# Taking VectorE out of half of the experts: the up product leaves PSUM on ScalarE and is multiplied in on GpSimd

## What is computed

```python
x = x + attention(layernorm(x))
xf = layernorm(x)                                   # (2048, 128)
weights, idx = gate(xf)                             # softmax, groups of 4, top 2 of 16 experts
combine = (one_hot(idx, 16) * weights[..., None]).sum(1)
h1 = einsum('td,edi->tei', xf, We1) + be1           # 16 experts, 64 wide
h3 = einsum('td,edi->tei', xf, We3) + be3
h = silu(h1) * h3
y = einsum('te,ted->td', combine, einsum('tei,eid->ted', h, We2) + be2)
z = (silu(xf @ ws1 + bs1) * (xf @ ws3 + bs3)) @ ws2 + bs2   # shared experts
x = x + y + z
```

## Time and profile before

| | |
|---|---|
| median of 3 runs | 423.87 us (423.43 to 426.72) |
| the profiled execution's own time | 423.36 us |
| its span, first to last instruction | 421.6 us |
| PE busy | 355.5 us, 84% |
| DVE busy | 311.8 us, 74% |
| ACT busy | 265.1 us, 63% |
| POOL busy | 202.1 us, 48% |
| mean granted TensorE clock | 0.931 of full |

### The profile page before, as it was taken

The page is one execution under the profiler, slowest core; times in us unless marked ns, Lnnn a source line. Parts: engine busy times, 40 slices in busy tenths (PEclk is TensorE's granted clock), DMA queues, the critical chain, the costliest instruction groups (busy, mean ns, idle before and its releaser), DMA issues.

```text
span 421.6 us, 7243 instructions
## 1 busy us (share of the span) xinstructions
PE 355.5 (84%) x2489; PEld 135.9 (32%) x2489; DVE 311.8 (74%) x595; ACT 265.1 (63%) x382; POOL 202.1 (48%) x283
## 2 busy tenths in 40 slices
PE   2743769688988998988789999997998999999796
PEld 2321333233442324322223233232323232434242
DVE  7694994989799997779965696659879336259664
ACT  2413258048779617965389748992884899996480
POOL 7611986786524896622412362311342522559432
PEclk9985659669999989999989999999999999999899
DMA  7232005000500620000290200000000000260171
GB/s 246 91 95 55 2 1 152 2 2 9 145 2 3 150 53 2 2 5 0 72 205 3 76 1 3 0 2 2 1 2 2 26 26 2 67 136 2 45 157 50
DMA packets 16869, 20.01 MB, mean 47 GB/s; under 512 B 1633, under 2 KB 12418, under 8 KB 16706
## 3 DMA queue, kind: packets, MB, share of 16 engines
q1 hardware_dynamic: 15298, 18.24, 17.2%
q10 hardware_dynamic: 1536, 1.31, 1.3%
HBM read 11.95 MB, written 1.18 MB: 31 GB/s over the span
## 4 chain that ended last, share of the span: by engine, by line
PE 46%; DVE 30%; ACT 9%; issue 7%; POOL 4%; DMA 2%; ACTq 1%; DVEq 0%; POOLq 0%
PE psum L986 11%; PE psum L1021 11%; DVE mx_diag L1494 11%; PE psum L966 7%; DVE mx_full L1494 6%; PE psum L1035 5%; ACT probs L1102 4%; PE psum L942 3%; PE psum L905 3%; DMA w_raw<-in_w_attn 2%; PE psum L914 1%; DVE mv L1573 1%; ACT mh L1170 1%; PE psum L936 1%; DMA k_st<-parts 1%
## 5 line engine op out<-in xcount | busy, mean ns | idle before, releaser
L1102 ACT ACTIVATE probs<-psum 128x1024 f32<-128x1024 f32 x144 | 141.0, 1026 | 39.4 <-PE psum L966 38.5
L1494 DVE TENSOR_REDUCE mx_diag<-psum 128x4 f32<-128x512 f32 (+2 forms) x96 | 96.4, 1039 | 29.4 <-PE psum L942 29.1
L1365 POOL TENSOR_TENSOR mh<-mh,mv 128x512 f32<-128x512 f32 x36 | 45.9, 1280 | 81.2 <-DVE mv L1573 81.0
L1494 DVE TENSOR_REDUCE mx_full<-psum 128x2 f32<-128x1024 f32 x64 | 75.6, 1216 | 12.3 <-PE psum L942 12.2
L1355 POOL TENSOR_SCALAR_AFFINE_SELECT probs<-probs 128x256 f32<-128x256 f32 (+1 forms) x112 | 47.7, 444 | 70.3 <-ACT probs L1102 69.0
L986 PE MATMUL psum<-probs,v_ones 128*9 128x512 f32 (+3 forms) x768 | 77.6, 494 | 2.2 <-POOL probs L1355 1.7
L1021 PE MATMUL psum<-x2T,experts 128*128 128x512 f32 x144 | 76.5, 639 | 3.0 <-ACT mv L1161 1.5
L942 PE MATMUL psum<-k_st,q_st 62*128 62x512 bf16 (+3 forms) x384 | 62.7, 358 | 3.9 <-DVE mx_full L1494 2.8
L966 PE MATMUL psum<-q_st,k_st 64*128 64x512 bf16 (+3 forms) x384 | 55.8, 338 | 10.5 <-ACT probs L1102 6.1
L936 PE MATMUL psum<-tabs 64*128 64x64 bf16 (+1 forms) x384 | 26.0, 215 | 21.2 <-DVE mx_diag L1494 8.3
L1573 DVE SCALAR_TENSOR_TENSOR mv<-psum,experts,mv 128x512 f32<-128x512 f32 x36 | 26.5, 745 | 23.3 <-ACT mh L1173 23.3
(11 more groups left out here) (163 smaller groups left out, 388.7 us busy)
## 6 DMA issues: line engine op xcount, KB each, us to landing
comb_b<-combine_scratch SPq DMA_DIRECT2D x32, 256.0 KB, 5.6
q_st<-parts SPq DMA_DIRECT2D x24, 128.0 KB, 2.5
k_st<-parts SPq DMA_DIRECT2D x18, 128.0 KB, 2.4
experts<-in_w_moe SPq DMA_DIRECT2D x1, 1737.0 KB
out<-xs SPq DMA_DIRECT2D x4, 256.0 KB, 2.2
xs<-in_x SPq DMA_DIRECT2D x3, 256.0 KB, 9.7
k_st<-parts ACTq DMA_DIRECT2D x6, 128.0 KB, 4.1
q_st<-maxT SPq DMA_DIRECT2D x32, 4.0 KB
```

The source lines that it names most:

```text
L1102: act.activation(probs[:, n % P_RING, :, :], wpair("scores", (s, i)), ACT.Exp, scale=SCALE).then_inc(exp_done, 1)
L1365: pool.tensor_tensor(t, t, mv[:, at % V_RING, :], ALU.mult).then_inc(gate_done, 1)
L1494: dve.tensor_reduce(dst[:, a % 2, qt, :, pairs[0]:pairs[0] + nm], w, AX.X, ALU.max, negate=True).then_inc(max_free, 1)
```

## The change

For the chunks in `GATED_ON_ACT` (0 and 1, so 18 of the 36 experts) stage `moe_a` leaves DVE. ACT reads u from its bank with an Identity activation that adds the bias, into a new ring `mu` of two buffers; this is now the bank's last read. A third ACT instruction per expert stands where `moe_a` stands in `SCHEDULE`, and it waits until `moe_g` of the expert two before is done, since that frees its buffer. POOL multiplies twice where it multiplied once: `mh` by `mv`, then, behind its own semaphore, `mh` by `mu`. To make room `T_RING` goes from 9 to 8. Chunks 2 and 3 are as before. `plan()` still takes `moe_a` for a stage of DVE, so `SCHEDULE` and the banks are what they were, entry for entry.

```diff
-P_RING, V_RING, T_RING = 6, 4, 9
+P_RING, V_RING, T_RING = 6, 4, 8
+GATED_ON_ACT = (0, 1)
+U_RING = 2
+        mu = sb("mu", [P, U_RING, CH])
+            def biased(x, n):
+                at = UNITS * x + n
+                if at >= U_RING:
+                    act.wait_ge(gate_done, at - U_RING + 1)
+                act.activation(mu[:, at % U_RING, :], wbank("moeU", (x, n)), ACT.Identity, bias=b1[:, unit(n):unit(n) + 1]
+                               ).then_inc(u_read, 1)
+
...
+                elif kind == "moe_a" and arg[0] in GATED_ON_ACT:
+                    biased(*arg)
...
                     pool.wait_ge(u_read, at + 1)
                     t = mh[:, at % T_RING, :]
-                    pool.tensor_tensor(t, t, mv[:, at % V_RING, :], ALU.mult).then_inc(gate_done, 1)
+                    if x in GATED_ON_ACT:
+                        pool.wait_ge(act_t, 2 * at + 2)
+                        link(pool.tensor_tensor(t, t, mv[:, at % V_RING, :], ALU.mult))
+                        pool.tensor_tensor(t, t, mu[:, at % U_RING, :], ALU.mult).then_inc(gate_done, 1)
+                    else:
+                        pool.tensor_tensor(t, t, mv[:, at % V_RING, :], ALU.mult).then_inc(gate_done, 1)
...
-                elif kind == "moe_a":
+                elif kind == "moe_a" and arg[0] not in GATED_ON_ACT:
                     gate_unit(*arg)
```

## The result

The changed kernel takes 447.84 us (median of 4 runs, 445.47 to 450.07), the kernel before 423.94 us beside it (423.43 to 426.72). The ratio is 1.055, with an interval of 1.051 to 1.059: 23.9 us slower. The forecast was 441 with a range of 432 to 448, so the sign is right and the time lies at the upper end of the range. About 7 us are missing in the sum, and what follows is as much about them as about the 17.8 that it had.

What follows compares the result with a forecast made beforehand. No engine bounds the kernel alone; the chain changes hands every few us. 2.7 + 5.0 + 2.0 + 4.0 + 4.1 = 17.8 us on a 421.6 span gave 439.4, then 441.2 as time; forecast 441, range 432 to 448.

Steps and rivals of the forecast that it cites:

- The price of one expert: From the end of `mu` to that of POOL's weighting 4.1 us; experts in a row on POOL 4.0 instead of 2.65.
- A: Chunk 0, experts 0 to 5 (137 to 186 us): +2.7 at the sum of (0,1), +5.0 by that of (0,4).
- B: Rest of chunk 0 (186 to 215 us): late `mu` holds PE, DVE takes part back; +2.0, ends -2.0 and +4.2.
- C: Chunk 1, experts 0 to 3 (236 to 268 us): 1.9 for (1,0) to (1,2), 2.2 for (1,3); together +4.0.
- D: Chunk 1, experts 4 to 6 (290 to 317 us): +4.1 at the sum of (1,6), including 1.2 at (1,4).
- E: Experts (1,7) and (1,8): DVE's lateness, which goes, covers the second product; 0 to within 0.3 us.
- What costs nothing: Chunks 2 and 3 unchanged, `T_RING` 8 leaves distance, and the `gate_done` wait ahead of `mu` is met in time for (0,5).
- added wait: Rival: the `gate_done` wait binds, routing is held, or PE's holes lower the clock; +4, so 445; chance 0.12.
- The rule on the port: Chunk 1's routing under POOL: five instructions held end it near 190, by the rule 191.5; the sum had 0 for it.
- Delays are taken back: Rival: saturated DVE recovers PE's lateness, B gives -2.0, C and D lose only plain products; 434.5; chance 0.14.
- Faster: Rival: PE has slack for every sum and DVE's product leaves the chain, some 5 us; 419; chance 0.03.
- no change: Rival: DVE's gain and POOL's loss cancel, which needs A under 5; chance 0.03.

Runs made afterwards that it cites:

- pool_twice: The kernel before with `T_RING` 8 and, in chunks 0 and 1, a second POOL product into a scratch tile: 445.20 us, ratio 1.051 to the kernel before.
- mu_early: The change with each `mu` instruction right behind the plus-one of its own expert on ACT: 438.55 us, ratio 1.036 to the kernel before.
- chunk 1 alone: The change for chunk 1 only, with chunk 0's nine experts left on DVE: 435.18 us, ratio 1.029 to the kernel before.
- fill_after: The change with PE products of zeros ahead of its wait at six expert sums: 440.64 us, ratio 1.038 to the kernel before.
- two_holds: The kernel before, `T_RING` 8, with an extra POOL product for (0,0) and (0,1): 428.95 us; its pair adds six zero products at (0,1): 425.12 us.
- chunk 0 alone: The change for chunk 0 only, with chunk 1's nine experts left on DVE: 437.07 us, ratio 1.033 to the kernel before.
- five_early: The scheme for experts (0,6), (0,7), (0,8), (1,0), (1,7) only, `mu` right behind the plus-one, others as before: 425.34 us, ratio 1.0035 to the kernel before.
- fill_one: The kernel before with `T_RING` 8 and three PE products of zeros at the sum of (0,1): 424.39 us, ratio 0.9998.
- fill_before: The kernel before with `T_RING` 8 and PE products of zeros, nearly all in the first 100 us, two at (0,1): 426.87 us, ratio 1.0066.

## Why the prediction came out as it did, by its own steps

**The price of one expert: right.** 4.0 us for experts in a row on POOL. The chain of the changed kernel in order of time (start us, us, what):

```profile
170.13 0.59 ACT mu L1171
...
170.78 1.28 POOL mh L1379
...
172.13 1.27 POOL mh L1380
173.48 1.27 POOL mh L783
174.74 1.24 POOL mh L1379
```

From the end of `mu` at 170.72 to that of the weighting at 174.75 are 4.03 us, and the next expert follows at once; the sums of (0,2), (0,3) and (0,4) start 3.98 and 3.92 apart.

**A, 2.7 + 5.0: right, 2.7 + 4.7.** The `mu` of (0,2) sits behind the tanh of (0,3), one `moe_v` later, just ahead of LayerNorm 2, and released POOL at 170.78. The forecast of 180.4 for the sum of (0,4) becomes 182.9 with the 1.4 of the start and the 1.1 of half clock at 155; it began at 182.70. But the reason given, the late place, is the smaller part. `pool_twice`, in which nothing waits for ACT's `mu` and no row of LayerNorm 2 was held (each took 0.16 or 0.17 us), was 7.8 late at (0,5), counted from its start and with half clock, the change 10.0. So the second product makes most of A by itself and the late place some 2 us. `mu_early` has 8.1: it is rid of the late place, but pays at LayerNorm 2 for the port.

**B, +2.0: right**, and neither of its ends. Nothing of DVE's saving showed in the delay.

**C, +4.0: right, 3.9**, and 3.9 with chunk 1 alone: 2.0 over (1,0) to (1,2), where 1.9 was taken, and 1.9 at (1,3), where 2.2 was. PE's row at 280.23 with its 2.13 of idle is that of (1,3).

**D, +4.1: 3.2** in the change, 3.6 in `fill_after`. Mis-sized by 0.5 to 0.9. What was too dear is ACT's way from one `mu` to the next. The forecast added up whole lengths, 4.75 us from the end of the `mu` of (1,5) to that of (1,6), but ACT's rows overlap: one of 0.68 is followed by the next after 0.57. The changed kernel took 4.31 (325.79 to 330.10). For LayerNorm 2 it was 1.54 instead of 1.64, and (1,4) lost 1.05 in `fill_after` instead of 1.2.

**E, 0: wrong, 1.9.** I took `mu` of (1,7) for one that follows its own tanh. ACT of the changed kernel:

```profile
345.04 0.69 ACT L1180 ACTIVATE mh<-psum,b1h 128x512 f32<-128x512 f32 x1 [1.80 <-PE psum L1024]
345.76 0.72 ACT L1183 ACTIVATE mh<-mh,ones_col 128x512 f32<-128x512 f32 x1
346.38 0.56 ACT L1251 COPY maxT<-psum 8x512 bf16<-8x512 bf16 x1
348.35 0.69 ACT L1164 ACTIVATE mv<-psum,b3h 128x512 f32<-128x512 f32 x1 [1.41 <-PE psum L1024]
348.93 0.68 ACT L1171 ACTIVATE mu<-psum,experts 128x512 f32<-128x512 f32 x1
```

It stands behind `moe_v` of (1,8), for which ACT itself waits 1.41 us for PE. The tanh was done at 346.5, `mu` only at 349.6, and three POOL products later PE, idle for 2.15, begins at 353.78. The place that was so carefully followed in A and C was not looked up here. Half clock behind it cost 2.8 more.

**What costs nothing: right.** The wait on `gate_done` did not bind (no `mu` row of the changed kernel has idle time ahead of it), and neither did the shorter ring (3.76 and 3.78 in `two_holds`).

**The sum, 17.8: the holds are 18.4** (17.1 by `fill_after`). The agreement is partly luck: 0.9 too much in D and 1.9 too little in E. There is also a slip in it: 439.4 of span plus 1.8 is the time of the profiled execution, 441.2, and with the 0.5 to the median 441.7.

**The clock, not in the sum: 7.0 us.** This is the step that failed: the sum had nothing for it. The trace of before has 0.62 in 152 to 156 us, but behind a wait for POOL of only 0.20 us, so it could not price a hold of 2 us. The "added wait" rival had the clock with two stretches and +4. In the change each of the four waits of about 2 us has half clock behind it (at (0,1) it is the one of before, made longer), and there is another at 309, ahead of which PE waited in pieces for DVE; the one at 211 went: +1.1, +1.4, +1.2, +2.8, +1.8, -1.3. `fill_after` shows that it comes with the holds and not with the product's work: with the waits left and the clock kept, 7.2 us are back. The pair of `two_holds` adds that filler works, with 1.1 us at its own place. It should have been a term of the sum, at 0 to 3 us for each hold of 2 us, and not a rival. The 441 and the 7.0 found here make 448, but no row of before gave that figure.

**The rule on the port: its price was right, its effect nil, where I looked.** The routing of chunk 1 in the changed kernel's DVE timeline:

```profile
180.09 1.30 DVE L1557 TENSOR_TENSOR lg<-lg,rowb 128x64 f32<-128x64 f32 x1
181.42 1.29 DVE L1561 TENSOR_TENSOR pair_sums<-lg 128x48 f32<-128x48 f32 x1
182.63 1.29 DVE L1562 TENSOR_TENSOR pair_sums<-lg 128x32 f32<-128x32 f32 x1
...
184.34 0.95 DVE L1572 TENSOR_TENSOR lg<-gsm 128x64 f32<-128x64 f32 x1
...
195.55 0.96 DVE L1511 TENSOR_REDUCE mx_diag<-psum 128x2 f32<-128x768 f32 x1 [3.38 <-PE psum L945]
```

Five instructions were held by about a microsecond each and the routing ended at 191.0. The prediction had 190 with five held and 191.5 by the rule; moved on by the 1.4 of the start these are 191.4 and 192.9, so five held rows it was, and not a stall for all of POOL's time. But DVE was soon waiting for PE again, 3.38 us, as the sum had it. Where the port does decide is LayerNorm 2, as `mu_early` shows; the prediction had not asked which chains of short DVE instructions lie under POOL once ACT is early.

**The rivals.** *Delays are taken back* fell: `two_holds` carries its delay through the saturated stretch to the end, and chunk 0 alone carries 13.7 us through the whole of chunk 1. *Faster* and *no change* fell with (0,1), whose sum waited 1.97 us, and in `five_early` DVE's relief, where it should have been worth most, did not even pay for what ACT and POOL had to take over. *An added wait* was right in one of its three causes, the clock, and too low in its price.

**The signs.** POOL's busy time rose by 22.8 (23 was said), ACT's by 10.7 (12), DVE's fell by only 7.9 (13): the instructions held by POOL eat part of what the 18 products gave. `pool_twice` shows this without the gift: DVE's work is that of before there, and its busy time rose from 311.8 to 316.1 us.

## What to carry to other kernels

An instruction that moves to another engine keeps its place in the order, and that place was made for the old engine; look up for each of them what now stands ahead of it, the last ones too. A busy share says nothing on this: POOL was idle for half of the span, and still its second product alone cost 21.8 us, because PE's sums wait for what stands behind it. When a hold of some 2 us on TensorE is added, put 0 to 3 us for the lower clock behind it into the sum, and look for chains of short DVE instructions that will then lie under POOL.

## What the runs showed of the hardware

- **Half clock behind a hold.** After its waits of 1.97 to 2.15 us PE of the changed kernel ran at half clock (0.50 to 0.58 in 4 us), two matmuls mostly in 2.07 us instead of 1.12, and lost 1.1 to 2.8 us in each stretch. It is no certain price: with chunk 1 alone a wait of 2.14 us had none (1.00 in 341 to 345 us). Behind the wait of 2.13 at 280.23 the first two matmuls still took 1.12 us and the clock fell within 2 us; behind those of 1.09, 0.89 and 0.88 us it did not fall anew. A stretch at 309 had no such wait ahead of it, but PE had been busy for only 2.17 of the 4 us before.
- **Zeros keep the clock.** Six bf16 products of zeros (1.47 us) within such a wait brought the clock of the next 5 us from 0.67 to 1.00. The kernel got 3.8 us back, 1.1 of them at that place and the rest later, for a reason that is not shown. `fill_one` got nothing back, and in `fill_before` such products cost 3.0 us net.
- **A POOL product holds one short DVE instruction to its own end.** 0.17 us become 1.1, and then a few pass until the next product. Ten of them in a row took 6.8 us instead of 1.9.
- **Executions start differently.** Ahead of any edit the profiled executions differed by up to 4 us (-0.8 to +3.2), so delays have to be counted from a place ahead of the first edit.
